# Other moments for the token shifts, the weight transfers and one residual sum in a twelve-layer transformer kernel

## The reference

```
x = x + 0.5 * ffn(layernorm(x));  x = x + attn(layernorm(x));  x = x + 0.5 * ffn(layernorm(x))
ffn: for i in range(6):
    x = attn_layer(shift_tokens(x), Wqkv[i], q_scale[i], k_scale[i], Wo[i]) + x
    x = ffn_layer(shift_tokens(x), ln_g[i], ln_b[i], W1[i], b1[i], W2[i], b2[i]) + x
shift_tokens(t): the second half of the channels comes from the token before
attn_layer: qkv = x @ Wqkv (128 -> 3*1024, 16 heads of 64); q, k = l2norm * scale, rotary tables;
            window 32: each query sees its window and the one before; out @ Wo
ffn_layer:  layernorm(x) @ W1 + b1 -> a, gate; (a * gelu(gate)) @ W2 + b2
```

## Time and profile before

| | |
|---|---|
| median of 3 runs | 3380.83 us |
| the profiled execution | 3380.69 us |
| its span | 3378.9 us |
| granted clock of TensorE | 0.994 |
| busy: TensorE, VectorE, ScalarE, GpSimd | 97%, 82%, 72%, 66% |

### The profile page before, as it was taken

The page is one execution under the profiler, slowest core; times in us unless marked ns, Lnnn a source line. Parts: engine busy times, 40 slices in busy tenths (PEclk is TensorE's granted clock), DMA queues, the critical chain, the costliest instruction groups (busy, mean ns, idle before and its releaser), DMA issues. The chain is left out here.

```text
span 3378.9 us, 150942 instructions
## 1 busy us (share of the span) xinstructions
PE 3288.9 (97%) x63515; PEld 2482.8 (73%) x63515; DVE 2758.7 (82%) x6952; ACT 2424.5 (72%) x3769; POOL 2227.0 (66%) x1454
## 2 busy tenths in 40 slices
PE   6999999999999999999999999999999999999998
PEld 3777777777777777777777777777777777777776
DVE  5788888888888888889998888888888888888885
ACT  2777777777777777777777777777777777777775
POOL 4666666666666666667888666666666666666663
PEclk7999999999999999999999999999999999999999
DMA  3111111111111111111111111111111111111111
GB/s 115 51 48 51 48 48 50 48 51 47 48 46 51 48 51 48 49 49 48 50 42 51 48 50 48 48 50 48 51 45 48 48 51 48 51 48 51 50 51 42
DMA packets 199180, 170.06 MB, mean 50 GB/s; under 512 B 139610, under 2 KB 172525, under 8 KB 198509
## 3 DMA queue, kind: packets, MB, share of 16 engines
q1 hardware_dynamic: 193901, 157.05, 17.1%
q10 hardware_dynamic: 4608, 3.34, 0.3%
HBM read 33.38 MB, written 1.05 MB: 10 GB/s over the span
## 5 line engine op out<-in xcount | busy, mean ns | idle before, releaser
L1112 POOL TENSOR_TENSOR rot<-rot,swp 128x1024 f32<-128x1024 f32 x384 | 907.4, 2363 | 140.0 <-DVE rot L901 140.0
L705 ACT ACTIVATE sq<-proj 128x512 f32<-128x512 f32 x768 | 437.7, 596 | 551.2 <-PE proj L503 540.0
L503 PE MATMUL proj<-wq,xsT 128*128 128x512 f32 x1536 | 772.4, 625 | 14.4 <-DVE rot L901 10.2
L1121 POOL TENSOR_TENSOR rot<-rot,rn 128x1024 f32<-128x1024 f32 x384 | 724.4, 1908 | 0.0
L1102 POOL TENSOR_TENSOR rt<-rt,half 128x1 f32<-128x1 f32 x192 | 105.3, 548 | 807.0 <-DVE rt L971 807.0
L895 DVE TENSOR_TENSOR swp<-proj,tab 128x512 f32<-128x512 f32 x768 | 522.6, 680 | 17.0 <-ACT sq L705 13.6
L901 DVE TENSOR_TENSOR rot<-proj,tab 128x512 f32<-128x512 f32 x768 | 519.7, 677 | 1.5 <-PE tps L514 1.5
L514 PEld LDWEIGHTS tps<-idf,rot 128*128 128x128 f32 x3072 | 360.2, 141 | 207.3 <-issue 203.4
L1025 DVE SCALAR_TENSOR_TENSOR hT<-proj,b1c,fg 114x128 f32<-114x128 f32 (+1 forms) x576 | 166.7, 345 | 419.7 <-ACT fg L769 414.2
L1106 POOL TENSOR_TENSOR prob<-prob,rr 128x1024 f32<-128x1024 f32 x192 | 365.4, 1903 | 186.0 <-DVE rr L983 186.0
L540 PEld LDWEIGHTS sps<-kT,qT 64*32 64x32 f32 x24576 | 366.0, 106 | 134.8 <-issue 134.4
(11 more groups left out here) (111 smaller groups left out, 5743.0 us busy)
## 6 DMA issues: line engine op xcount, KB each, us to landing
vb<-va SPq DMA_DIRECT2D x192, 384.0 KB, 3.5
vb<-va SPq DMA_DIRECT2D x192, 128.0 KB, 3.4
wq<-in_L_ffn_Wqkv SPq DMA_DIRECT2D x95, 192.0 KB
xs<-Z SPq DMA_DIRECT2D x384, 32.0 KB
xs<-Z SPq DMA_DIRECT2D x384, 28.0 KB
xs<-Z SPq DMA_DIRECT2D x384, 3.8 KB
xs<-Z SPq DMA_DIRECT2D x384, 0.2 KB
wo<-in_L_ffn_Wo SPq DMA_DIRECT2D x94, 64.0 KB
```

Source lines behind the costliest of these rows:

```text
L503: mm(proj[:, c % 2, :], xsT[:, k.parity(L_QKV), :], wq2[:, bass.ds(w + c * 512, 512)], start=True, stop=True).then_inc(p_qkv[c], 1)
L705: fn(sq[:, c * 512:(c + 1) * 512], proj[:, c % 2, :], ACT.Square).then_inc(a_sq[c], 1)
L1112: g_.tensor_tensor(r, r, swp[:, g * INNER:(g + 1) * INNER], ALU.add).then_inc(g_add[g], 1)
L1121: g_.tensor_tensor(r, r, rn[:, g * HEADS:(g + 1) * HEADS].unsqueeze(2) .to_broadcast([P, HEADS, DH]), ALU.mult).then_inc(g_nm[g], 1)
```

## The change

SP's step issues the value shift first and lets it wait for `p_O` (the attention product's end) instead of `a_oT`. The input shift is now that of tile `s + 1` (lag L_DX = -1) and stands behind the value shift, then the weights, then the second shift. The shift of tile 0 stands ahead of the pipeline. On VectorE Wo's sum goes from behind `rsqrt(k, 4)` to behind the row sum of k's squares.

```diff
+L_DX = -1
@@ SP, step @@
-                if k.on(L_X):
-                    k.wait(v_z, L_X)
-                    k.wait_mid(m_z, TILES)
-                    if k.reg is None:
-                        k.wait(p_xT, L_X + 2)
-                    shift(k, L_X, xs[:, k.parity(L_X), :], d_xs[k.parity(L_X)])
                 if k.on(L_SM):
-                    if k.reg is None:
-                        k.wait(a_v[0], L_SM)
-                    k.wait(a_oT, L_SM + 1)
+                    k.wait(a_v[0], L_SM)
+                    k.wait(p_O, L_AV)
                     par = k.parity(L_SM)
                     sp.dma_start(vb[WIN:P, :], va[0:P - WIN, par, :]).then_inc(d_vb, 16)
                     sp.dma_start(vb[0:WIN, :], va[P - WIN:P, 1 - par, :]).then_inc(d_vb, 16)
+                next_tile(k)
+                load_weights(k)
                 if k.on(L_WO):
                     k.wait(v_z1, L_WO)
                     shift(k, L_WO, xs2[:, :], d_xs2)
-                load_weights(k)
...
+            def next_tile(k):
+                if k.on(L_DX):
+                    k.wait(v_z, L_DX)
+                    k.wait_mid(m_z, TILES + L_DX)
+                    k.wait(p_xT, L_X + 1)
+                    shift(k, L_DX, xs[:, k.parity(L_DX), :], d_xs[k.parity(L_DX)])
             sp.wait_ge(c_zero2, 1)
+            next_tile(Step(sp, None, L_DX, {}))
             pipeline(sp, step, between, mid_end=N + TILES, end=OUT - 1, last=OUT + TILES)
@@ VectorE, step @@
                     v.tensor_reduce(xsq[:, HEADS:2 * HEADS], heads(sq[:, INNER:2 * INNER]), AX, ALU.add).then_inc(v_red[1], 1)
+                if k.on(L_WO):
+                    k.wait(p_wo, L_WO)
+                    k.wait(a_xn, L_WO + 1)
+                    k.wait_pair(d_xs, L_WO - 1, 64)
+                    zs = Z[:, bass.ds(k.slot(L_WO), P)]
+                    v.tensor_tensor(zs, zs, ops[:, 0, 0:P], ALU.add).then_inc(v_z1, 1)
+                if k.on(L_QKV):
                     rotate(k, 3, False)
                     rsqrt(k, 1)
                     rotate(k, 2, True)
                     rsqrt(k, 2)
                     rotate(k, 2, False)
                     rsqrt(k, 4)
-                if k.on(L_WO):
-                    k.wait(p_wo, L_WO)
-                    k.wait(a_xn, L_WO + 1)
-                    k.wait_pair(d_xs, L_WO - 1, 64)
-                    zs = Z[:, bass.ds(k.slot(L_WO), P)]
-                    v.tensor_tensor(zs, zs, ops[:, 0, 0:P], ALU.add).then_inc(v_z1, 1)
```

## The result

The changed kernel took 3416.61 us (median of 4 runs, 3410.98 to 3421.05), the kernel before 3381.26 us beside it (3379.4 to 3383.32): a ratio of 1.0108, 95% interval [1.0094, 1.0123]. Slower, by some 35 us. The forecast was 3407, with a range of 3370 to 3432.

A forecast was written before the change was run, and what follows sets the result against it. TensorE, busy 97% of the span, was taken as the bound, with VectorE's list up to the last straight product nearly so. 3380.7 + 40 (sum) - 12 (holes) + 0.5 (start) - 2 (stalls) = 3407 us, range 3370 to 3432.

The forecast's parts named there:

- The signs named beforehand: L509 waits naming L901 in most steps, sum ahead of the product by 0.2 or near 0.45 us, scores' "issue" 120 to 134.
- The race between VectorE and TensorE: VectorE's last straight product frees `proj` half 0 just in time for TensorE's `values(k, 0)`; product 0.20 or 0.47 us later.
- The sum's term: Wo's sum ahead of the straight products delays TensorE's values in 171 steps by 0.235 us each: +40 us, from 31 to 50.
- The second rival: The race has more slack than read, first term at most 10 us: 3374, between 3367 and 3383; chance 0.13.
- The 17 steps of the middle layer: Two more matmuls ahead of the values on TensorE cover the later product in these steps, so they cost nothing.
- the earlier half's product: `proj`'s half for `values(k, 1)` would be free at 1018.08, over 1.1 us ahead of 1019.25: no wait there.
- The code's holes: Gaps in the scores from TensorE's code fetches; moved transfers give back less than a quarter of some 54 us: -12 us.
- The first rival: Transfers from 1023.24 on and the second shift's tail delay the scores' code fetch; all 54 us return: 3365, chance 0.17.
- The start: k's first weights go out near 14 instead of 7.73, landing near 18 against 17.86: +0.5 us, from 0 to +3.
- The absorbed stalls: TensorE stalls ahead of the values, mostly L555's holes, fall into a wait that is there anyway: -2 us.
- Value shift: Waiting for `p_O`, it goes out near 1012.4 instead of 1014.34 but is read in the next step: nothing.
- The second shift and the order of SP's queue: Second shift some 2 us earlier, its VectorE reader not waiting; SP's queue has time for the moved transfers: nothing.

The follow-up runs named there:

- value shift alone: The kernel before with only the value shift's wait changed to the attention product's end, and the wait for `a_v[0]` in every step; ratio 1.0003.
- twice the weights: The kernel before with each steady weight transfer issued again into a tile nobody reads; ratio 1.0008 in both runs.
- transfers alone: The changed kernel with Wo's sum back in its old place, SP's new order kept; 3372.19 us against 3372.77, ratio 1.0001.
- products first: The kernel of two buffers with `rsqrt(k, 1)` and `rsqrt(k, 2)` moved behind the last straight product; 3381.5 us, ratio 0.9990 to the kernel before.
- best of the parts: The kernel of transfers alone, start mended, with three short inverse-root instructions behind the last straight product; 3370.07 us against 3377.12 before, ratio 0.9975.
- transfers alone, start mended: The kernel of transfers alone with step 0's weights for k and v issued ahead of tile 1's shift; 3370.57 us, ratio 0.9994 to the kernel before.
- behind the product for 3: The changed kernel with Wo's sum one instruction later, behind `rotate(k, 3, False)`; 3393.55 us, ratio 1.0070 to the kernel before.
- two buffers: The changed kernel with two buffers for the second shift, so the sum waits for the normalisation one tile earlier; 3400.3 us, ratio 1.0044 to before.
- sum alone: The kernel before with only Wo's sum moved behind the row sum of k's squares, SP's order old; 3418.38 us, ratio 1.0140.
- the pair on one chip: Both kernels unchanged, profiled again on one chip: before 3382.36 us in that execution, after 3419.46, ratio 1.0113.
- the pair of the prediction: The first profiles of the two unchanged kernels: before in an execution of 3380.69 us, and the changed kernel, measured at ratio 1.0108.
- the first four experiments: The runs transfers alone, sum alone, behind the product for 3, and transfers alone, start mended; ratios 1.0001, 1.0140, 1.0070 and 0.9994.

## Why the prediction was right, and where its sum was wrong

The holes of the scores (us, and how many), and VectorE's lateness (the wait of the values' load for the straight product):

| kernel | transfers | sum | holes | wait for VectorE |
|---|---|---|---|---|
| before, two executions | old | old | 53.9 (60), 48.6 (54) | 8.4, 8.4 |
| value shift alone | old | old | 49.9 (56) | 8.0 |
| twice the weights | old, doubled | old | 51.0 (60) | 8.4 |
| transfers alone | new | old | 47.6 (58) | 8.9 |
| products first | new | early, covered | 49.3 (54) | 5.8 |
| best of the parts | new | old | 50.2 (58) | 2.1 |
| transfers alone, start mended | new | old | 42.8 (53) | 8.5 |
| behind the product for 3 | new | middle | 44.2 (58) | 43.4 |
| two buffers | new | early | 42.4 (50) | 50.0 |
| sum alone | old | early | 41.1 (47) | 74.2 |
| after, two executions | new | early | 38.7 (45), 39.6 (47) | 74.8, 74.4 |

- **The signs named beforehand came:** the values' loads wait for the straight product in most steps, the sum stands ahead of it, 0.2 us in one kind of step and 0.47 in the other. The scores' "issue" at 118.8 is just under the 120 to 134 given.
- **The race between VectorE and TensorE: right.** The last straight product came 0.20 and 0.47 later, to the hundredth; the waits that name it stand in 191 steps. The matmul moved by 0.12 and 0.27, inside the intervals given (0.09 to 0.20, 0.27 to 0.38).
- **The sum's term: +40 forecast, 39 to 48 measured.** By the pair on one chip, the mean of the 171 steady steps without the scores' own stretch grew by 0.23 us, by the pair of the prediction by 0.28; x 171 = 39 and 48. The medians by kind of step, 0.19 and 0.34, give 45, and the sum alone cost 46. What made the 0.235 low is that I took the middle between "the matmul keeps its 0.10 behind the load" and "it starts with the load". It does start with the load in the record, but what follows is timed from the load, so the load's own 0.21 and 0.38, near my upper ends, were nearly the whole answer. The place and the wait for `a_xn` each make about half: with two buffers the wait's part goes, 19 us by the medians, 25 us with the sum behind the product for 3. The second rival (more slack) falls.
- **The 17 steps of the middle layer, put at nothing: some 2 us.** In them the load of `values(k, 0)` came 0.16 us later on average (2.6 and 3.0 us in all), so the two more matmuls cover the product only in part of them.
- **Two slips in the working.** I wrote that TensorE's entries name no engine; the wait list has 8.4 us at L509 and 59.7 at L503 that name L901, as shown above. And I compared the earlier half's product (1018.08) with 1019.25, which is the load of `values(k, 0)`. The load of `values(k, 1)` stands at 1018.27 in the same trace, 0.19 behind 1018.08. After shows what that was worth: product's end 1029.23 + 0.68 = 1029.91, load at 1030.11. Free, as stated, but by 0.2 us and not by over 1.1.
- **The code's holes: -12 forecast, -10 and -17 measured, for another cause.** This step of the prediction failed, and that its number came near is luck. The scores' stretch is 0.06 us a step shorter by the pair on one chip, 0.10 by the pair of the prediction. But the table sorts the holes by VectorE's lateness more than by the transfers. With the old transfers they are 50.9 on average in time (four executions) and 41.1 late; with the new ones 47.5 in time (four kernels) and 39.2 fully late (two executions), 42 to 44 half late. So the lateness is worth 8 to 10 us and the transfers 2 to 3, and that is less than the spread of the four kernels with new transfers (42.8 to 50.2). The chips differ in this too, so look at one: before 48.6, products first 49.3, two buffers 42.4, after 39.6, in the order of the lateness. On the chip of the first four experiments the gap is small: 47.6 and 42.8 in time, 41.1 late. What the lateness does to a hole wasn't measured by itself: I think that TensorE, held before the values, gives a fetch under way time to land, so that a part of the wait is paid back. That would explain the order of the table; it isn't shown.
- **The first rival (transfers delay the fetch): refuted** by the packets and holes of products first against before, on one chip.
- **The start: +0.5 forecast (0 to +3), +3.1 and +3.6 measured** by the first maximum of the two pairs. The landing was mis-sized, not the mechanism. One trace says little here: over all traces with the old order of the start the first maximum stands at 45.2 to 47.2 us, with the new one at 48.1 to 50.0.
- **The absorbed stalls, -2:** L555's "issue" was 36.1 and is 36.2, in the other pair 38.6 and 35.9. Nothing, or too little to tell.
- **Value shift:** nothing, as forecast. The second shift and the order of SP's queue were run only together with the rest of the transfers, and show nothing there.

By the pair on one chip: 39 - 10 + 3.6 = 33, and 2 from the middle layer's steps, where the spans differ by 35.5. The forecast of 3407 was 10 us low, from small terms with one sign: up to 8 in the sum, 3 at the start, 2 in the stalls and 2 in the middle layer's steps.

What stays open: the sum alone came out at 1.0140 and the sum with the transfers at 1.0113 and 1.0108; the interval of the first touches that of the second and not quite that of the third. Either the transfers give back some 9 us when VectorE is late, or it is the difference of chips; no single chip ran both. The chips can do it: two buffers and the sum behind the product for 3 have the same transfers and the same lateness of the product (11.73 and 11.72 us), and came out at 1.0044 on one chip and 1.0070 on the other, as far apart as 1.0113 and 1.0140 on the same two. The holes (41.1 against 38.7 and 39.6) speak for 2 us.

## What to carry to other kernels

Where two engines finish a step within 0.1 us of each other, price an edit by what it puts ahead of the instruction that gives the shared buffer free, and count the waits that it brings: here a 0.29 us sum cost some 0.13 us a step by its place and as much again by a wait met in every second one. The remedy is the same reading turned round: put short work that nobody waits for behind that instruction, and give the overwritten tile a second buffer. And before calling a change of a stall's total a gain, look at how much it differs between two executions of the unchanged kernel. Take the suspected cause away once, or add to it, and check in the packet records that the edit reached the stretch in question: my doubled weights went past it.

## What the runs showed of the hardware

- The handover from VectorE to a waiting weight load took 0.06 us (1031.40 to 1031.46 in after), and the matmul behind such a load is recorded as starting with it; behind a load that didn't wait it starts 0.11 later (1030.11 and 1030.22 in the steady rows of after).
- VectorE's instructions overlap: the sum of 0.29 us takes 0.20 from start to start, ahead of a product (1029.03 and 1029.23 in after) as well as ahead of the root's steps.
- A hole in the scores ends 1.39 us after the end of the last code fetch before it (median of 60 in the trace of before, 80% within 1.29 to 1.51; 1.37 to 1.42 in the other twelve traces), while the fetch itself takes 1.0 to 1.1 (medians). A hole is 0.8 to 0.9 us long in the median, and 0.5 to 1.3 in most cases.
- 256 KB more in every second step, 16% on top of what queue q1 moves (24.7 of 157.05 MB), cost TensorE nothing that could be measured; they ran behind the scores.
- Other transfers beside a code fetch made no difference to the holes that could be told: 54 holes of 48.6 us with packets in flight beside all 54 fetches (before), 54 holes of 49.3 us with packets beside 2 (products first), on one chip.
